# Two-layer attention and mixture-of-experts kernel: score groups placed together in the first attention, scores placed last in each step of the second

## The chip, the cores and the metric

The kernel runs on one core of a Trainium2 chip. The metric is device time in microseconds of one execution; the time of the kernel before is the median of three runs. A profile of one further execution shows what each engine did: TensorE (PE, with its weight loads as PEld), VectorE (DVE), ScalarE (ACT), GpSimd (POOL) and the DMA queue of SyncE (SP).

## What is computed

The input x is (2, 1024, 128) float32. Four blocks follow, each added to x. The two attentions are what the change touches; cut to what matters:

```python
x = x + attn0(layernorm(x)); x = x + moe(layernorm(x))
x = x + attn1(layernorm(x)); x = x + channel_mix(layernorm(x))

def attn0(X):                       # 16 heads, d = 64, 1024 tokens, 2 batch elements
    Q1, Q2, K1, K2 = halves of X @ Wq[h] and X @ Wk[h]; V = X @ Wv[h]
    P = softmax(Q1 @ K1.T * s) - lam * softmax(Q2 @ K2.T * s)
    O = P @ V                       # then Y = concat(O) @ Wo + bo, layer norm, * 0.2

def attn1(x):                       # 16 heads, d = 8, same tokens, masked keys
    O = softmax(Q @ K.T * s) @ V; return O @ Wo.T + bo
```

## The kernel before, in words

Each engine runs a list of instructions in a fixed order, written out by hand; semaphores tie them together. PSUM has eight banks of 512 float32 columns. In both attentions six banks hold scores, in turn in three pairs; the other two are `TRB`/`OT` (bank 6) and `MISC` (bank 7).

**First attention.** An item is one head of one batch element (32 of them, n = 2h + b), and `heads` runs the function `item` of each engine over them, with one more before and after. An item has eight steps s, each for 128 queries. A score group (`scores`, L1209 and L1210) is six fp16 matmuls on half the rows of the array, two at a time, into a pair of banks, once for p = 0 (the first softmax) and once for p = 1. For each, VectorE takes the negated row maximum (`maximum`, L825) and ScalarE the exponent with its row sum (`exponent`, L649). VectorE's `weigh` (L832, L834) works out the factor rho of the step before, and GpSimd (`subtract`, L511 and L513) scales the second softmax and subtracts it. Three steps later TensorE transposes the difference in two halves (`turn`, L1221, four 128x128 transposes each into bank 6), and ScalarE copies each half out (`keep_t`, L660). `turn` waits for the copy before it, since there is one bank.

Everything else of TensorE goes through MISC, in pieces named `first_misc` and `second_misc`: `values` (P times V, L1232), `to_out` (output projection, L1241), and the projections for the next item, `project_q` (L1245), `project_k` (L1251), `project_v` (L1259). Their users are on the other engines: `high` (ScalarE, L670) and `low` (VectorE, L842) split Q and K in two fp16 halves, `keep_v` (L866) keeps V, `normalise` (L850) divides the values' result, `add_out` (L860) adds the output. Since there is one MISC, each piece waits until the piece before has been read: in step 2 the second piece waits for `low` 0, in steps 5, 6, 7 for `low` 1, 2, 3; the first piece of step 1 and the second of step 4 wait for `normalise`; the first pieces of steps 5, 6, 7 for `add_out`, `keep_v` and `keep_v`; the first of step 2 for `add_out`.

VectorE's order in a step, which the change leaves alone, is: `normalise` (s = 1), `add_out` (s = 5) or `keep_v` (s = 6, 7); maximum of p = 0; `weigh`; `add_out` (s = 1), `normalise` (s = 4) or `low` (s = 2, 5, 6, 7); maximum of p = 1. ScalarE's order is: `high` (s = 2, 5, 6, 7), the copy of the first turn, exponent 0, the copy of the second turn, exponent 1.

TensorE's order in a step is:

```python
scores(n, b, u3, s, 0)
first_misc(h, b, s)
turn(..., 0)
scores(n, b, u3, s, 1)
turn(..., 1)
second_misc(h, b, s)
```

SyncE's queue carries the swap of QT's halves (`swap_q`, after `low` 0 and `low` 3), the reciprocal sums on their way over DRAM (`spread_r`) and the weights of the next head.

**Second attention.** A block n is four heads of one batch element, eight blocks of 32 steps t. In each step TensorE issues `maxima1` (L1463) for the next block, whose row maxima VectorE takes (L1110), and `scores1` (L1446) for this one, whose exponents ScalarE takes (L759); both are two fp16 matmuls into one pair of banks, and they take the three pairs in turn. So `maxima1` waits for the exponent of two steps before and `scores1` for the maximum of the step before. In odd steps `values1` (L1477, eight matmul records) follows for two steps that are done; it waits for the exponent of two steps before, and at t = 3 and t = 19 also for ScalarE's copy of `OT` (L737). At t = 3 and 19 come four small transposes (`spread1`, L1484), at t = 14 and 30 the output projection (`to_out1`, L1489). The block n = -1 has maxima only, the last block scores only; there `scores1` waits for the exponent of three steps before.

Of the kernel before, what the change touches and what calls it, by code (L numbers as in the profile page):

```python
# [28 lines left out]
def two_layers(nc, a, out):  # L29
    ctx = ExitStack()  # L30
    with ctx:
# [262 lines left out]
        def flags(h, b):  # L294

            if isinstance(h, int):
                n = 2 * h + b
                return 0 <= n - 1 < last0, 0 <= n < last0, 0 <= n + 1 < last0
            return True, True, True

        def at_least(eng, done, count):
            if not isinstance(count, int) or count > 0:
                eng.wait_ge(done, count)
# [314 lines left out]
        def _(act):  # L618
# [24 lines left out]
            def exponent(n, u3, s, p):  # L643
                u = 16 * n + 2 * s + p
                bank = 2 * ((u3 + 2 * s + p) % 3)
                act.wait_ge(s_max, u + 1)
                if p == 0:
                    at_least(act, s_tr_mm, 2 * (8 * n + s) - 6)
                A.activation((E1, E2)[p][s % 4], PS[:, bank:bank + 2, :].rearrange("p a b -> p (a b)"), ACT.Exp,  # L649
                             bias=nmx[:, 2 * s + p:2 * s + p + 1], scale=1.0,  # L650
                             accum_out=sums[:, s, p:p + 1]).then_inc(s_exp, 1)
# [20 lines left out]
            def item(h, b, u3):  # L672
                prv, own, nxt = flags(h, b)
                n = 2 * h + b
                for s in range(8):
                    if s == 1 and nxt and b == 1:
                        at_least(act, s_lo_ok, 4 * (n + 1))
                        A.activation(bcur[:, :], bqk[:, bass.ds(h + 1, 1), :].rearrange("p o i -> p (o i)"),
                                     ACT.Copy).then_inc(s_bc_ok, 1)
                    if s in (2, 5, 6, 7) and nxt:  # L680
                        high(n + 1, 1 - b, (2, 5, 6, 7).index(s), h + b + 1)
                    later = own if s >= 3 else prv
                    if later:
                        keep_t(n if s >= 3 else n - 1, (s + 5) % 8, 0)
                    if own:
                        exponent(n, u3, s, 0)
                    if later:
                        keep_t(n if s >= 3 else n - 1, (s + 5) % 8, 1)
                    if own:
                        exponent(n, u3, s, 1)  # L690

            heads(act, item)

            CT16 = MISC.bitcast(F16)[:, 0:HF]
# [464 lines left out]
        def _(pe):  # L1159
# [34 lines left out]
            def scores(n, b, u3, s, p):  # L1194


                u = 16 * n + 2 * s + p
                bank = 2 * ((u3 + 2 * s + p) % 3)
                if s == 0 and p == 0:
                    pe.wait_ge(s_lo_ok, 4 * n + 3)  # L1200
                    pe.wait_ge(s_qx_dma[0], 32 * (n + 1))
                if s == 4 and p == 0:
                    pe.wait_ge(s_lo_ok, 4 * n + 4)
                    pe.wait_ge(s_qx_dma[1], 32 * (n + 1))
                at_least(pe, s_exp, u - 2)
                top, bottom = (QT[b], QX[b]) if p == 0 else (QX[b], QT[b])
                q = slice(s * 128, s * 128 + 128)
                for j, (ql, kl) in enumerate(((0, 0), (0, 1), (1, 0))):
                    MM(PS[:, bank, :], top[0:64, ql, q], KT[b][0:64, p, kl, :], start=(j == 0), stop=(j == 2))  # L1209
                    mm = MM(PS[:, bank + 1, :], bottom[64:128, ql, q], KT[b][64:128, p, kl, :], start=(j == 0),  # L1210
                            stop=(j == 2))
                mm.then_inc(s_fill, 1)
# [49 lines left out]
            def first_misc(h, b, s):  # L1262
                prv, own, nxt = flags(h, b)
                n, m, p = 2 * h + b, 2 * h + b + 1, 1 - b
                if s == 0 and prv:
                    values(n - 1, p, 0, 2)
                if s == 1 and prv:
                    to_out(h + b - 1, n - 1, 0)
                if s == 2 and nxt:
                    at_least(pe, s_y_ok, 2 * n - 1)  # L1270
                    at_least(pe, s_lo_ok, 4 * m)
                    project_q(h + b, m, p, 0)
                if s == 3 and prv:
                    values(n - 1, p, 1, 1)
                if s == 4 and prv:
                    values(n - 1, p, 1, 3)
                if s == 5 and nxt:
                    at_least(pe, s_y_ok, 2 * n)
                    at_least(pe, s_lo_ok, 4 * m + 1)
                    project_k(h + b, m, p, 0)  # L1280
                if s == 6 and nxt:
                    pe.wait_ge(s_v_ev, 2 * m + 1)
                    project_k(h + b, m, p, 1)
                if s == 7 and nxt:
                    pe.wait_ge(s_v_ev, 2 * m + 2)
                    project_q(h + b, m, p, 1)

            def second_misc(h, b, s):
                prv, own, nxt = flags(h, b)
                n, m, p = 2 * h + b, 2 * h + b + 1, 1 - b  # L1290
                if s == 0 and prv:
                    values(n - 1, p, 0, 3)
                if s == 2 and prv:
                    pe.wait_ge(s_y_ok, 2 * n - 1)
                    if nxt:
                        pe.wait_ge(s_lo_ok, 4 * m + 1)
                    values(n - 1, p, 1, 0)
                if s == 3 and prv:
                    values(n - 1, p, 1, 2)
                if s == 4 and prv:  # L1300
                    to_out(h + b - 1, n - 1, 1)
                if s in (5, 6) and nxt:
                    pe.wait_ge(s_lo_ok, 4 * m + s - 3)
                    project_v(h + b, m, p, s - 5)
                if s == 7 and own:
                    at_least(pe, s_y_ok, 2 * n)
                    if nxt:
                        pe.wait_ge(s_lo_ok, 4 * m + 4)
                    values(n, b, 0, 0)
                    values(n, b, 0, 1)  # L1310

            def item(h, b, u3):
                prv, own, nxt = flags(h, b)
                n = 2 * h + b
                for s in range(8):
                    later = own if s >= 3 else prv
                    if own:
                        scores(n, b, u3, s, 0)
                    first_misc(h, b, s)
                    if later:  # L1320
                        turn(n if s >= 3 else n - 1, (s + 5) % 8, 0)
                    if own:
                        scores(n, b, u3, s, 1)
                    if later:
                        turn(n if s >= 3 else n - 1, (s + 5) % 8, 1)
                    second_misc(h, b, s)

            heads(pe, item)


# [156 lines left out]
            def to_out1(hf):  # L1487
                pe.wait_ge(s_on1_ok, hf + 1)
                MM(MISC, wo1[:, hf // 4, :], on[:, :], start=True, stop=True).then_inc(s_y1_mm, 1)  # L1489

            for n in range(-1, last1 + 1):
                own, nxt = 0 <= n < last1, n + 1 < last1
                for t in range(32):
                    if nxt:
                        maxima1(n + 1, t)
                    if own:
                        scores1(n, t)
                    if t == 1 and n >= 1:
                        values1(n - 1, 15)
                    if t % 2 == 1 and t > 1 and own:  # L1500
                        values1(n, t // 2 - 1)
                    if t == 3 and own:
                        if n >= 1:
                            pe.wait_ge(s_yc1_ok, 2 * n - 1)
                        spread1(2 * n + 1)
                    if t == 14 and n >= 1:
                        if own:
                            pe.wait_ge(s_ct_ev1, 2 * n + 2)
                        to_out1(2 * n - 1)
                    if t == 19 and nxt:  # L1510
                        if n >= 1:
                            pe.wait_ge(s_yc1_ok, 2 * n)
                        spread1(2 * (n + 1))
                    if t == 30 and own:
                        if nxt:
                            pe.wait_ge(s_ct_ev1, 2 * (n + 1) + 1)
                        to_out1(2 * n)


            pe.wait_ge(s_y1_ok, 4 * G1)  # L1520
# [55 lines left out]
```

## Time and profile before

| | before |
|---|---|
| median of 3 runs | 1957.23 us |
| lowest, highest | 1950.94, 1958.64 us |
| the profiled execution | 1955.24 us |
| its span | 1953.4 us |
| mean granted TensorE clock | 0.938 |
| busy TensorE, VectorE | 1628.1 us (83%), 1444.0 us (74%) |
| busy ScalarE, GpSimd | 1262.6 us (65%), 974.4 us (50%) |

The first attention lies from about 58 to 1262 us of the span, the second from about 1465 to 1897 us. Busy shares over the whole span hide that the two are bound by different things; the rows below show them one by one. The ends of matmuls are modelled, so the start of the next instruction is the better mark of when TensorE was free.

### The profile page before, as it was taken

To read this page: it belongs to the slowest core of one execution; us is meant where nothing else is said; L and a number is where in the kernel's file an instruction comes from. 1 tells how busy PE (TensorE), PEld (TensorE's weight loads), DVE (VectorE), ACT (ScalarE), POOL (GpSimd) and SP (SyncE) were. 2 spreads that over 40 slices of the span, in tenths; PEclk is the share of its full clock that TensorE was granted. 3 is DMA by queue.
4 is the path that set the end of the run, shared out by engine and by line. 5 is a ranking of instruction groups with operands and counts; after the bars stand their busy time and mean duration, and the time that the engine had idled before them with its cause. 6 is when DMAs were issued, how large, how long until landed. Compare 5 with 4: busy or idle time off the path is not lost.

```text
span 1953.4 us, 27210 instructions
## 1 busy us (share of the span) xinstructions
PE 1628.1 (83%) x9867; PEld 661.5 (34%) x9867; DVE 1444.0 (74%) x2199; ACT 1262.6 (65%) x2078; POOL 974.4 (50%) x637
## 2 busy tenths in 40 slices
PE   2899999999999999999999999833576777777763
PEld 1334444444434443444443444322441111111112
DVE  2678777777777877777777777596679777777608
ACT  1677777777777777777777777611052777777751
POOL 1577777777777777777777777720000011111110
PEclk8899999999999999999999999965685999999986
DMA  3111111111111111111111111000010000000000
GB/s 95 31 28 33 33 33 33 33 28 33 33 33 32 31 30 38 29 30 35 28 33 38 28 33 29 17 2 0 1 38 1 7 13 13 12 13 13 13 18 22
DMA packets 68107, 50.82 MB, mean 26 GB/s; under 512 B 27187, under 2 KB 56918, under 8 KB 67974
## 3 DMA queue, kind: packets, MB, share of 16 engines
q1 hardware_dynamic: 67974, 49.07, 11.1%
q8 instruction: 80, 1.31, 0.3%
q14 instruction: 53, 0.43, 0.1%
HBM read 28.79 MB, written 1.31 MB: 15 GB/s over the span
## 4 chain that ended last, share of the span: by engine, by line
PE 62%; issue 14%; DVE 13%; ACT 6%; POOL 2%; SPq 2%; DMA 0%; POOLq 0%; ACTq 0%; DVEq 0%
PE PS L1209 15%; PE PS L1221 14%; PE PS L1232 13%; DVE mxp L1110 4%; PE PS L1251 4%; PE PS L1241 3%; PE PS L1259 3%; ACT ering L649 3%; ACT va L660 2%; PE PS L1245 2%; DVE on L850 2%; PE PS L1477 2%; PE PS L1422 2%; DVE st L797 1%; POOL on L574 1%
## 5 line engine op out<-in xcount | busy, mean ns | idle before, releaser
L825 DVE TENSOR_REDUCE nmx<-PS 128x1 f32<-128x1024 f32 x512 | 625.4, 1222 | 212.1 <-PE PS L1210 206.1
L513 POOL TENSOR_TENSOR ering<-ering 128x1024 f32<-128x1024 f32 x256 | 603.7, 2358 | 21.4
L649 ACT ACTIVATE ering<-PS,nmx 128x1024 f32<-128x1024 f32 x512 | 572.6, 1118 | 2.9 <-DVE nmx L825 2.1
L511 POOL TENSOR_SCALAR ering<-ering,rho 128x1024 f32<-128x1024 f32 x256 | 286.6, 1119 | 300.9 <-DVE rho L834 300.9
L1209 PE MATMUL PS<-region 64*128 64x512 f16 x1536 | 420.4, 381 | 1.0 <-ACT ering L649 1.0
L1210 PE MATMUL PS<-region 64*128 64x512 f16 x1536 | 420.4, 381 | 0.0
L1110 DVE TENSOR_REDUCE mxp<-PS 128x2 f32<-128x1024 f32 x256 | 302.8, 1222 | 79.1 <-PE PS L1463 79.0
L1221 PE MATMUL PS<-ident,ering 128*128 128x128 f32 x2048 | 330.6, 284 | 11.4 <-ACT t L660 2.5
L759 ACT ACTIVATE ering<-PS 128x1024 f32<-128x1024 f32 x256 | 259.3, 1025 | 108.8 <-PE PS L1446 107.9
L1221 PEld LDWEIGHTS PS<-ident,ering 128*128 128x128 f32 x2048 | 222.0, 140 | 303.1 <-POOL ering L513 99.1
L660 ACT ACTIVATE t<-PS 128x512 f32<-128x512 f32 x256 | 152.6, 596 | 88.7 <-PE PS L1221 88.7
L1209 PEld LDWEIGHTS PS<-region 64*128 64x128 f16 x1536 | 105.4, 94 | 243.4 <-issue 96.8
L660 ACT ACTIVATE va<-PS 128x512 f32<-128x512 f32 x128 | 76.3, 596 | 131.9 <-PE PS L1221 131.9
L670 ACT ACTIVATE region<-PS,bcur 128x512 f16<-128x512 f32 x128 | 88.3, 690 | 93.6 <-PE PS L1251 50.8
L1477 PE MATMUL PS<-ering,acc 128*32 128x512 f32 x1024 | 137.3, 608 | 7.3 <-ACT osb L737 3.5
L842 DVE SCALAR_TENSOR_TENSOR region<-PS,bcur,region 128x512 f16<-128x512 f32 x128 | 96.1, 751 | 53.8 <-ACT region L670 46.6
L1232 PE MATMUL PS<-t,vslot 128*64 128x512 f32 x512 | 130.8, 611 | 0.0
L574 POOL TENSOR_TENSOR on<-osb,rcp 128x512 f32<-128x512 f32 x16 | 20.4, 1272 | 221.4 <-DMA rcp<-scr 221.4
L1446 PE MATMUL PS<-region 64*128 64x512 f16 x256 | 50.1, 388 | 86.2 <-DVE mxp L1110 74.6
L649 ACT ACTIVATION_READ_ACCUMULATOR ering<-PS,nmx 128x1 f32 x512 | 106.4, 208 | 0.0
L1210 PEld LDWEIGHTS PS<-region 64*128 64x128 f16 x1536 | 105.6, 95 | 0.0
L1245 PE MATMUL PS<-xT,wq_s 128*128 128x512 f32 x128 | 73.9, 660 | 14.5 <-POOL wq_s L504 14.0
(251 smaller groups left out, 1708.7 us busy)
## 6 DMA issues: line engine op xcount, KB each, us to landing
region<-region SPq DMA_DIRECT2D x128, 128.0 KB, 2.3
osb<-scr SPq DMA_DIRECT2D x32, 256.0 KB, 4.1
rcp<-scr SPq DMA_DIRECT2D x32, 256.0 KB, 4.1
rcp<-scr SPq DMA_DIRECT2D x64, 64.0 KB, 2.0
x<-in_L_attn_X SPq DMA_DIRECT2D x4, 256.0 KB, 3.7
wq_raw<-in_L_attn_Wq SPq DMA_DIRECT2D x16, 64.0 KB, 2.5
wk_s<-in_L_attn_Wk SPq DMA_DIRECT2D x16, 64.0 KB, 1.8
wo_s<-in_L_attn_Wo SPq DMA_DIRECT2D x32, 32.0 KB, 3.2
```

Of the source, the lines that this page charges most:

```text
L511: P.tensor_scalar(e2, e2, rho[:, s:s + 1], 1.0, ALU.mult, ALU.mult).then_inc(s_scl_ok, 1)
L513: P.tensor_tensor(e1, e1, e2, ALU.subtract).then_inc(s_sub_ok, 1)
L649: A.activation((E1, E2)[p][s % 4], PS[:, bank:bank + 2, :].rearrange("p a b -> p (a b)"), ACT.Exp, bias=nmx[:, 2 * s + p:2 * s + p + 1], s ...
L660: A.activation(PT[half][i][:, :, (s % 4) * 128:(s % 4) * 128 + 128], TRB.rearrange("p (k q) -> p k q", k=4), ACT.Copy).then_inc(s_tr_ev, 1)
L759: A.activation(ering[:, c % 8, :, :], PS[:, at:at + 2, :], ACT.Exp, scale=SCALE1).then_inc(s_exps1, 1)
L825: V.tensor_reduce(nmx[:, 2 * s + p:2 * s + p + 1], PS[:, bank:bank + 2, :].rearrange("p a b -> p (a b)"), AX.X, ALU.max, negate=True).then ...
L1110: V.reduce_max(part[:, hp:hp + 3:2, qt, kh:kh + 1], PS[:, at:at + 2, :], AX.X).then_inc(s_maxed1, 1)
L1209: MM(PS[:, bank, :], top[0:64, ql, q], KT[b][0:64, p, kl, :], start=(j == 0), stop=(j == 2))
L1210: mm = MM(PS[:, bank + 1, :], bottom[64:128, ql, q], KT[b][64:128, p, kl, :], start=(j == 0), stop=(j == 2))
L1221: mm = TR(TRB[:, j * 128:j * 128 + 128], E1[s % 4][:, k * 128:k * 128 + 128], ident[:, :])
L1232: mm = MM(MISC[64 * c:64 * c + 64, :], vslot[:, b, k, :], PT[half][k // 4][:, k % 4, :], start=(j == 0), stop=(j == 3))
L1477: mm = MM(OT[32 * i:32 * i + 32, :], vst[:, n % 2, k, i, :], ering[:, c % 8, i // 2, :], start=(k == 0), stop=(k == 7))
```

## The change

Three edits. On TensorE in the first attention a step is now first piece, score group 0, score group 1, turn 0, second piece, turn 1. On ScalarE both exponents stand between the copies of the two turns. On TensorE in the second attention the scores of a step come behind its values, its small transposes and its output projection. No instruction is added or removed.

```diff
--- before.py
+++ after.py
@@ -684,10 +684,9 @@
                         keep_t(n if s >= 3 else n - 1, (s + 5) % 8, 0)
                     if own:
                         exponent(n, u3, s, 0)
+                        exponent(n, u3, s, 1)
                     if later:
                         keep_t(n if s >= 3 else n - 1, (s + 5) % 8, 1)
-                    if own:
-                        exponent(n, u3, s, 1)
 
             heads(act, item)
 
@@ -1314,16 +1313,15 @@
                 n = 2 * h + b
                 for s in range(8):
                     later = own if s >= 3 else prv
+                    first_misc(h, b, s)
                     if own:
                         scores(n, b, u3, s, 0)
-                    first_misc(h, b, s)
+                        scores(n, b, u3, s, 1)
                     if later:
                         turn(n if s >= 3 else n - 1, (s + 5) % 8, 0)
-                    if own:
-                        scores(n, b, u3, s, 1)
+                    second_misc(h, b, s)
                     if later:
                         turn(n if s >= 3 else n - 1, (s + 5) % 8, 1)
-                    second_misc(h, b, s)
 
             heads(pe, item)
 
@@ -1493,8 +1491,6 @@
                 for t in range(32):
                     if nxt:
                         maxima1(n + 1, t)
-                    if own:
-                        scores1(n, t)
                     if t == 1 and n >= 1:
                         values1(n - 1, 15)
                     if t % 2 == 1 and t > 1 and own:
@@ -1515,6 +1511,8 @@
                         if nxt:
                             pe.wait_ge(s_ct_ev1, 2 * (n + 1) + 1)
                         to_out1(2 * n)
+                    if own:
+                        scores1(n, t)
 
 
             pe.wait_ge(s_y1_ok, 4 * G1)
```

## Rows read from the trace of the kernel before

**Rows 1.** Windows: stretch, length, busy (instructions) of PE, PEld, DVE, ACT, POOL, clock, DMA.

```profile
95.00:1208.00 1113.00, 1094.58 (x6629) 458.00 (x6630) 862.68 (x1244) 844.71 (x1553) 827.12 (x489) 1.00 0.15 32
601.07:638.60 37.53, 36.91 (x225) 15.40 (x224) 29.09 (x42) 28.53 (x53) 28.02 (x18) 1.00 0.14 35
1465.00:1500.00 35.00, 19.79 (x70) 3.56 (x66) 34.77 (x32) 1.87 (x2) 0.52 (x2) 0.50 0.00 1
1500.00:1870.00 370.00, 274.90 (x1984) 63.99 (x1982) 270.73 (x255) 268.25 (x286) 45.44 (x65) 0.99 0.05 12
```

**Rows 2.** Chain of waits, one step of the first attention: start, length, what.

```profile
622.86 0.43 PE PS L1221 x4
623.29 0.32 PE PS L1209
...
623.62 0.21 PE PS L1209
...
624.05 0.59 PE PS L1221 x4
```

**Rows 3.** Order of time, end of step 3, step 4: start, length, engine, line, operation.

```profile
633.01 1.08 PE L1232 MATMUL PS<-acc,vslot 128*64 128x512 f32 x4
...
634.02 0.39 PE L1209 MATMUL PS<-region 64*128 64x512 f16 x1
...
634.88 1.23 DVE L825 TENSOR_REDUCE nmx<-PS 128x1 f32<-128x1024 f32 x1 [1.13 <-PE PS L1210]
...
636.22 0.27 DVE L834 TENSOR_SCALAR rho<-sums,rr,cols 128x1 f32<-128x1 f32 x1
...
636.41 1.11 DVE L850 TENSOR_TENSOR on<-PS,rcp 128x512 f32<-128x512 f32 x1
...
637.62 1.08 PE L1241 MATMUL PS<-on,wo_s 128*128 128x512 f32 x2
...
638.63 0.39 PE L1209 MATMUL PS<-region 64*128 64x512 f16 x1
...
638.74 0.69 DVE L860 TENSOR_TENSOR yT<-yT,PS 128x512 f32<-128x512 f32 x1
```

**Rows 4.** Order of time, step 5 of the item before: low, maximum, projection, keep_v.

```profile
603.70 0.75 DVE L842 SCALAR_TENSOR_TENSOR region<-PS,bcur,region 128x512 f16<-128x512 f32 x1 [0.22 <-ACT region L670]
...
604.37 1.22 DVE L825 TENSOR_REDUCE nmx<-PS 128x1 f32<-128x1024 f32 x1
...
604.70 1.00 PE L1259 MATMUL PS<-wv_s,xT 128*128 128x64 f32 x8
...
605.74 0.42 DVE L866 TENSOR_TENSOR vslot<-PS,bv_b 128x256 f32<-128x256 f32 x1 [0.16 <-PE PS L1259]
```

**Rows 5.** Order of time, step 3: turn, its copy, the next turn.

```profile
631.08 0.66 PE L1221 MATMUL PS<-ident,ering 128*128 128x128 f32 x4
...
631.77 0.60 ACT L660 ACTIVATE t<-PS 128x512 f32<-128x512 f32 x1 [1.43 <-PE PS L1221]
...
632.42 0.66 PE L1221 MATMUL PS<-ident,ering 128*128 128x128 f32 x4
```

**Rows 6.** Order of time, second attention, one pair of steps.

```profile
1661.60 0.39 PE L1446 MATMUL PS<-region 64*128 64x512 f16 x2 [0.90 <-DVE mxp L1110]
...
1661.92 1.07 PE L1477 MATMUL PS<-ering,acc 128*32 128x512 f32 x8
1662.04 1.02 ACT L759 ACTIVATE ering<-PS 128x1024 f32<-128x1024 f32 x1 [0.48 <-PE PS L1446]
...
1662.92 0.39 PE L1463 MATMUL PS<-region,t 64*128 64x512 f16 x2
...
1663.35 2.36 DVE L1110 TENSOR_REDUCE mxp<-PS 128x2 f32<-128x1024 f32 x2 [0.52 <-PE PS L1463]
...
1664.64 0.39 PE L1446 MATMUL PS<-region 64*128 64x512 f16 x2 [0.89 <-DVE mxp L1110]
```

**Rows 7.** Order of time, second attention: copy of OT; exponents of the last block.

```profile
1654.99 0.59 ACT L737 ACTIVATE osb<-PS 128x512 f32<-128x512 f32 x1
...
1872.13 10.19 ACT L759 ACTIVATE ering<-PS 128x1024 f32<-128x1024 f32 x11 [0.56 <-PE PS L1446]
```

## The prediction

> **What bounds the kernel now.** I read the busy time by stretch first. In the steady part of the first attention TensorE is busy for 1094.6 of 1113 us at full clock, and one item (one head of one batch element, eight steps) takes 37.53 us, with TensorE busy for 36.91, VectorE for 29.1, ScalarE for 28.5 and GpSimd for 28.0 [rows 1]. So TensorE has next to no gap, and what counts for this part is two things: how long its instructions are, and whether the new order makes it wait. In the second attention no engine is full (275, 271 and 268 of 370 us): it is bound by a loop of waits. Then I read the chain of waits for what a piece of TensorE work costs behind another, and the order of time of single steps for the distance from each producer to its consumer.
>
> **Part 1, what the new order saves.** A step has two score groups (half-array fp16 matmuls), two turns (four full-array transposes each) and up to two pieces in the shared bank MISC. Four transposes cost 0.43 us behind full-array work and 0.59 behind score matmuls; the first score matmul costs 0.32, the ones behind it 0.21 [rows 2]. So a change of kind costs 0.11 to 0.16. I counted the changes in an item from the code: before (score, first piece, turn, score, turn, second piece) 41, after (first piece, score, score, turn, second piece, turn) 29. 12 x 0.14 = 1.7 us an item, 52 us over some 31 items. The Trainium skill says the same in "TensorEngine Tiling (Array Packing)", under "Key Properties": a change of tiling mode drains the array. By that rule alone the kernel would get faster; the trace agrees that the change of kind costs time.
>
> **Part 2, what the new order makes late.** VectorE's order is not touched: first maximum, the two small sums' operations, then (in seven of eight steps) one product for MISC's user, then the second maximum. Before the change TensorE had the first piece, a turn, the second score group and a turn between the first score group and the second piece, so the product was ready in time. I take step 4: score group at 634.02, its maximum at 634.88, rho at 636.22, the product `on` at 636.41 to 637.52, and the projection that needs it at 637.62, which is 3.6 us behind the score group's start and cost TensorE nothing [rows 3]. Now only the second score group and one turn stand between. I set up the step from its first score group at 0: second group at 0.74, turn at 1.38, its end 1.97. VectorE's product starts at 2.39 as before. A `low` takes 0.75 and so frees the second piece at 3.2 [rows 4]; a normalise takes 1.11 and frees it at 3.6 [rows 3]. TensorE stands still for 1.2 or 1.6 us, and everything it would have done then is queued behind. Step by step, in TensorE time from first score group to first score group:
> - Steps 5 and 6: the value projection waits for `low` until 3.2; it takes 0.84 to 1.0, the turn 0.43. Meanwhile the second maximum (from 3.06) and keep_v (0.42) end at 4.7, and the next first piece waits for keep_v because it reuses MISC. Plus 1.0 for that piece (the value group of [rows 3] takes 1.01): 5.7 each [rows 4].
> - Step 7: `low` until 3.2, two value groups of about 0.93, turn 0.59, the next value group 1.01: 6.65.
> - Step 0: one value group and both turns end at 3.57, but to_out now is the first piece of step 1 and needs normalise, which stands behind the second maximum (from 2.39 to 3.6) and ends at 4.7. Plus 1.0: 5.7.
> - Step 1: no second piece, so the second turn must wait for ScalarE's copy of the first, 1.34 after the first turn's start [rows 5]; with the query projection 4.1.
> - Step 2: `low` again, about 0.1 later since ScalarE is behind: 5.9.
> - Step 3 has no such piece and only saves: 4.6.
> - Step 4: to_out waits until 3.6, takes 1.0; the second maximum, then the addition (0.69) that frees MISC for the key projection end at 5.4. Plus 1.0: 6.45.
>
> The sum is 44.8 us an item against 37.53, the 1.7 already in it, so 7.3 more. The first item has no earlier item's pieces and the last no projections: about 3 us each. 30 x 7.3 + 6 = **225 us more**. Covers that are gone are named above. POOL: a difference is used a whole step after it is ready (on the engine's own rows it idles about a quarter of each item), so longer steps only give it room; no DMA is issued earlier or later against its user, and the swap of QT has a step and more of room. ScalarE has 28.5 us of work an item, 3.6 a step [rows 1], below every new step; only behind the short step 1 is it late, which is in the sum of step 2. Both banks' exponents of the step before are done when the score groups want their banks: nothing. Unknown is how exactly a stopped TensorE restarts; between nothing and the 0.2 us by which the loads of weights in these rows precede a restart, on six stops. I take nothing for the centre and widen by 0.25 a stop either way: 6 x 0.25 x 30 = 45 us.
>
> **Part 3, the second attention.** Two steps (even, odd) take 3.03 us: maxima group of the even step at 1662.92, its maximum from 1663.35, the odd step's scores at 1664.64 once that bank is read, then the values group (0.31 behind), and the next maxima group 1.00 later [rows 6]. In the new order the values group no longer stands behind that wait; the scores stand behind the values. The loop is now: end of the odd exponent, 0.05, maxima group, 0.32, values, 1.00, scores, 0.44, exponent, 1.02 = 2.83 [rows 6], 0.20 less for a pair. Against this: at t=3 and t=19 values wait for ScalarE's copy of OT (0.59 [rows 7]) and are followed by the small transposes, and the scores now stand behind all of it: about 1.4 more than a plain pair where before it was 0.4. At t=14 and t=30 to_out is before the scores, 0.28 against 0.1. A block of 16 pairs: 16 x 2.83 + 2 x 1.4 + 2 x 0.28 = 48.6, before 16 x 3.03 + 0.8 + 0.2 = 49.5. Seven blocks: -6 us. The last block has no maxima and ScalarE is its bound: 11 exponents in 10.19 us, 1.85 a pair [rows 7]. There the new loop (0.05 + 1.00 + 0.44 + 1.02 = 2.5) is the longer: 13 plain pairs x 0.65, about 8 us more. **Together +2**, between -6 (the last block hides it) and +15.
>
> **Sum.** The profiled execution took 1955.24 us (span 1953.4); 1955.2 + 225 + 2 = 2182; the median of the runs shown, 1957.23, is 2 above it. I say 2183. About 0.5% is what a measurement of this kernel can tell from no change.
>
> **Rivals.**
> - **The saved changes of kind win.** If the products were ready at 1.97 after the first score group, 52 us fall off TensorE: about 1905. It decides at the second piece of steps 2, 4, 5, 6 and 7; it holds only if VectorE finished its product 2.0 after that score group, and the rows have 3.1 and 3.5. Chance 0.04.
> - **Half of it is absorbed**: the stops in steps 0 and 5, 6 (the waits for keep_v and normalise at the head of the next step) vanish, because VectorE can start earlier than I think. Then some 3.5 us an item remain: 2065 to 2110. VectorE's idle time speaks for it, its fixed order against it. Chance 0.07.
> - **The clock falls.** Before the second attention TensorE, busy for 19.8 of 35 us, was granted 0.50; in it, 74% busy, 0.99 [rows 1]. New items are 80% busy with gaps up to 1.6 us, so I expect full clock. If it fell for good, its some 36 us of work an item would double: above 2800. If it fell only in the last block, 10 us. Chance of the first 0.03.
> - **More delay than I wrote**, through ScalarE in steps 1 and 2: 2250 to 2330. Chance 0.08.
> - The forecast: 0.78.
>
> **Range and chances.** The likeliest case with its bounds: 2183 - 45 - 6 and + 45 + 15, which is 2132 to 2243. It leaves about 0.2 out. Faster by over 0.5%: 0.04, the first rival. Within: 0.01. Slower: 0.95.
>
> **What the next profile would show.** An item of about 44.8 us; in it second pieces idle behind `low` (L842) and `on` (L850) for 1.2 and 1.6 us; TensorE about 80% busy in the first attention; VectorE and ScalarE with the same busy totals; the score groups six in a row with one 0.32; second attention pairs of 2.83 and, in the last block, 2.5. Wrong would be an item under 42 or over 48, or stops at other places than those listed.

## The result, and the profile after

The changed kernel takes 2202.35 us, median of four runs (2198.6 to 2213.89), the kernel before 1956.9 (four runs): ratio 1.126, 95% interval 1.124 to 1.128. It is 245 us slower. The profiled execution took 2204.14 us, its span is 2202.3. Two executions lie far above all others, 2879.72 us of the kernel with TensorE's order alone and 3144.76 us of the kernel before, and they are left out of every comparison.

| us | before | after | difference |
|---|---|---|---|
| start to the first transposes behind the first attention | 1268.4 | 1518.3 | +249.9 |
| from there to the first maximum of the second attention | 196.8 | 186.0 | -10.8 |
| from there to the last block's first scores | 383.5 | 375.8 | -7.7 |
| last block, first to last scores | 34.0 | 50.7 | +16.7 |
| the rest of the span | 70.7 | 71.5 | +0.8 |

The second line holds work that the change does not touch. The middle is the same in all the kernels compared here, and in their profiles this line came out between 186.0 and 197.2 us, so I do not count the 10.8 us as an effect of the change.

Windows of the changed kernel (stretch, length, busy and instructions of PE, PEld, DVE, ACT, POOL, granted clock, DMA share, GB/s): one item, the steady first attention, a stretch with a dip of the clock, and two stretches of the last block of the second attention.

```profile
711.25:756.56 45.31, 36.95 (x227) 15.95 (x226) 28.37 (x42) 29.64 (x53) 28.08 (x17) 1.00 0.13 28
95.00:1400.00 1305.00, 1067.86 (x6414) 457.40 (x6410) 813.32 (x1205) 847.45 (x1505) 799.93 (x473) 0.99 0.12 27
...
813.00:815.00 2.00, 2.00 (x6) 0.28 (x6) 0.00 (x0) 1.34 (x4) 0.80 (x1) 0.50 0.06 14
...
2085.00:2106.00 21.00, 17.45 (x75) 2.87 (x76) 0.25 (x1) 11.04 (x12) 1.27 (x1) 0.52 0.06 14
2106.00:2113.00 7.00, 4.28 (x28) 0.64 (x26) 0.00 (x0) 5.58 (x8) 1.27 (x1) 0.97 0.00 0
```

Against [rows 1]: an item is 45.31 us instead of 37.53 (37.62 when it is counted before, too, from score group to score group), and the busy times of the four engines in it are within 1.2 us of what they were. So the work has not grown; TensorE stands still. Who it waits for is in the waits of TensorE (engine and line waited for: us in total, times, longest):

```profile
PE PS L1240 <- DVE on L849: 77.6, 64, 1.5
PE PS L1258 <- DVE region L841: 73.1, 64, 1.6
...
PE PS L1231 <- issue: 34.5, 32, 1.2
...
PE PS L1231 <- ACT va L660: 25.8, 29, 0.9
PE PS L1220 <- ACT va L660: 22.0, 32, 0.7
```

L1240 is `to_out`, L1258 `project_v`, L1231 `values`, L1220 `turn`. In the kernel before `to_out` waited 16.2 us for the product in 33 places and `project_v` 3.1 us in 2; now it is 77.6 and 73.1 in 64 each. The two lines for `values` name "issue" and ScalarE, but they stand in steps 7 and 2, where the code's other wait is for `low` (VectorE); what is named had long been done (in step 7 `low` ends at 726.06 and `values` starts at 726.16). Together these waits for VectorE's products are some 211 us; `turn` waits 42 us for ScalarE's copies. Now the same step as in [rows 3], in order of time:

```profile
704.81 0.39 PE L1208 MATMUL PS<-region 64*128 64x512 f16 x1
...
705.68 1.23 DVE L824 TENSOR_REDUCE nmx<-PS 128x1 f32<-128x1024 f32 x1 [1.85 <-PE PS L1209]
...
707.20 1.07 DVE L849 TENSOR_TENSOR on<-PS,rcp 128x512 f32<-128x512 f32 x1
...
708.20 1.21 DVE L824 TENSOR_REDUCE nmx<-PS 128x1 f32<-128x1024 f32 x1
...
708.33 1.13 PE L1240 MATMUL PS<-on,wo_s 128*128 128x512 f32 x2 [1.46 <-DVE on L849]
...
709.50 0.69 DVE L859 TENSOR_TENSOR yT<-yT,PS 128x512 f32<-128x512 f32 x1
...
710.24 1.08 PE L1250 MATMUL PS<-xT,wk_s 128*64 128x512 f32 x4 [0.34 <-DVE yT L859]
...
711.25 0.39 PE L1208 MATMUL PS<-region 64*128 64x512 f16 x1
```

The distance from the score group's start to `on`'s start is 2.39 us, as before (704.81 to 707.20). But TensorE arrives early: it stood idle for 1.46 us before the output projection, which starts 3.52 us behind the score group (+3.52), and the key projection behind it waits for the addition, so that the next step starts at +6.44. Step 5, against [rows 4]:

```profile
713.64 0.74 DVE L841 SCALAR_TENSOR_TENSOR region<-PS,bcur,region 128x512 f16<-128x512 f32 x1
...
714.43 1.10 PE L1258 MATMUL PS<-wv_s,xT 128*128 128x64 f32 x8 [1.13 <-DVE region L841]
...
715.38 0.61 PE L1220 MATMUL PS<-ident,ering 128*128 128x128 f32 x4
...
715.58 0.42 DVE L865 TENSOR_TENSOR vslot<-PS,bv_b 128x256 f32<-128x256 f32 x1
...
716.06 1.08 PE L1250 MATMUL PS<-xT,wk_s 128*64 128x512 f32 x4
...
717.07 0.39 PE L1208 MATMUL PS<-region 64*128 64x512 f16 x1
```

`low` starts 2.39 us behind the score group (711.25), and TensorE stands idle for it before the value projection. Then `keep_v`, behind the second maximum, sets the start of the next piece. The step is 5.82 us. Score groups do not wait here: in the whole execution they do so twice, 1.6 us together, both in the first item.

The pair of steps of the second attention, against [rows 6]:

```profile
1901.72 0.39 PE L1461 MATMUL PS<-region 64*128 64x512 f16 x2 [0.69 <-ACT ering L758]
...
1902.04 1.06 PE L1475 MATMUL PS<-ering,acc 128*32 128x512 f32 x8
...
1903.04 0.39 PE L1444 MATMUL PS<-region 64*128 64x512 f16 x2
...
1903.47 1.94 ACT L758 ACTIVATE ering<-PS 128x1024 f32<-128x1024 f32 x2 [0.89 <-PE PS L1444]
...
1904.55 0.39 PE L1461 MATMUL PS<-region 64*128 64x512 f16 x2 [0.69 <-ACT ering L758]
```

From one maxima group of an odd step (L1461) to the next it is 2.83 us; a pair took 3.03 before. What the group waits for is the exponent; before, `scores1` waited for the maximum. The last block, first at half clock, then at full clock:

```profile
2099.00 1.94 PE L1475 MATMUL PS<-ering,acc 128*32 128x512 f32 x8 [0.69 <-ACT ering L758]
...
2100.87 0.61 PE L1444 MATMUL PS<-region 64*128 64x512 f16 x2
...
2101.51 1.94 ACT L758 ACTIVATE ering<-PS 128x1024 f32<-128x1024 f32 x2 [1.66 <-PE PS L1444]
...
2102.59 1.94 PE L1475 MATMUL PS<-ering,acc 128*32 128x512 f32 x8 [0.69 <-ACT ering L758]
...
2119.59 1.07 PE L1475 MATMUL PS<-ering,acc 128*32 128x512 f32 x8 [0.90 <-ACT ering L758]
...
2120.59 0.39 PE L1444 MATMUL PS<-region 64*128 64x512 f16 x2
...
2122.10 1.06 PE L1475 MATMUL PS<-ering,acc 128*32 128x512 f32 x8 [0.90 <-ACT ering L758]
```

A pair takes 3.59 us in the first stretch (2099.00 to 2102.59) and 2.51 in the second (2119.59 to 2122.10). In both, values, scores and one exponent stand one behind the other, so TensorE's instructions are in the pair at full length: from values to scores it is 1.87 us at half clock and 1.00 at full clock.

### The profile page after: what moved, and what is told of

It reads as the page before. It is cut to its first block, busy times and chain, and to the rows that moved or that the text cites. A ratio compares the mean times of both kernels' runs of the same rounds, so it can differ in the third digit from the quotient of the medians.

```text
span 2202.3 us, 27210 instructions
## 1 busy us (share of the span) xinstructions
PE 1639.2 (74%) x9867; PEld 669.8 (30%) x9867; DVE 1428.4 (65%) x2199; ACT 1285.5 (58%) x2078; POOL 973.5 (44%) x637
## 4 chain that ended last, share of the span: by engine, by line
PE 44%; DVE 30%; issue 18%; ACT 4%; POOL 2%; SPq 1%; DMA 0%; POOLq 0%; DVEq 0%; ACTq 0%
DVE nmx L824 12%; PE PS L1231 10%; PE PS L1208 10%; PE PS L1220 5%; PE PS L1258 3%; PE PS L1240 3%; PE PS L1250 3%; DVE on L849 3%; DVE region L841 2%; PE PS L1244 2%; DVE yT L859 2%; DVE mxp L1109 2%; PE PS L1475 2%; ACT ering L758 2%; PE PS L1420 1%
## 5 line engine op out<-in xcount | busy, mean ns | idle before, releaser
L649 ACT ACTIVATE ering<-PS,nmx 128x1024 f32<-128x1024 f32 x512 | 568.2, 1113 | 89.2 <-DVE nmx L824 87.1
L1208 PE MATMUL PS<-region 64*128 64x512 f16 x1536 | 383.5, 384 | 1.6 <-ACT ering L649 1.6
L1209 PE MATMUL PS<-region 64*128 64x512 f16 x1536 | 383.5, 384 | 0.0
L1220 PE MATMUL PS<-ident,ering 128*128 128x128 f32 x2048 | 331.1, 284 | 41.8 <-ACT va L660 22.0
L1109 DVE TENSOR_REDUCE mxp<-PS 128x2 f32<-128x1024 f32 x256 | 310.7, 1225 | 62.8 <-PE PS L1461 55.3
L758 ACT ACTIVATE ering<-PS 128x1024 f32<-128x1024 f32 x256 | 252.9, 1021 | 134.2 <-PE PS L1444 134.0
L1220 PEld LDWEIGHTS PS<-ident,ering 128*128 128x128 f32 x2048 | 221.5, 143 | 281.9 <-issue 195.8
L1208 PEld LDWEIGHTS PS<-region 64*128 64x128 f16 x1536 | 126.2, 95 | 332.8 <-ACT ering L649 149.0
L1475 PE MATMUL PS<-ering,acc 128*32 128x512 f32 x1024 | 143.3, 633 | 28.5 <-ACT osb L736 11.7
L1231 PE MATMUL PS<-t,vslot 128*64 128x512 f32 x512 | 131.0, 609 | 34.2 <-issue 33.1
L1240 PE MATMUL PS<-on,wo_s 128*128 128x512 f32 x128 | 72.0, 645 | 77.6 <-DVE on L849 77.6
L1258 PE MATMUL PS<-wv_s,xT 128*128 128x64 f32 x512 | 72.4, 286 | 73.1 <-DVE region L841 73.1
L1209 PEld LDWEIGHTS PS<-region 64*128 64x128 f16 x1536 | 126.2, 95 | 0.0
L1461 PE MATMUL PS<-region 64*128 64x512 f16 x256 | 53.8, 417 | 72.9 <-ACT ering L758 65.2
```

Of the source, the lines that this page charges most:

```text
L758: A.activation(ering[:, c % 8, :, :], PS[:, at:at + 2, :], ACT.Exp, scale=SCALE1).then_inc(s_exps1, 1)
L1109: V.reduce_max(part[:, hp:hp + 3:2, qt, kh:kh + 1], PS[:, at:at + 2, :], AX.X).then_inc(s_maxed1, 1)
L1220: mm = TR(TRB[:, j * 128:j * 128 + 128], E1[s % 4][:, k * 128:k * 128 + 128], ident[:, :])
L1231: mm = MM(MISC[64 * c:64 * c + 64, :], vslot[:, b, k, :], PT[half][k // 4][:, k % 4, :], start=(j == 0), stop=(j == 3))
L1475: mm = MM(OT[32 * i:32 * i + 32, :], vst[:, n % 2, k, i, :], ering[:, c % 8, i // 2, :], start=(k == 0), stop=(k == 7))
```

## The experiments

Both halves of the change were run, each single move of the first attention, and remedies for the wait that it brought. "Groups" are the two score groups of a step, "pieces" the MISC work, and each kernel differs from the kernel before by the diff shown, unless said otherwise. Repeated arguments are cut to `...` in the diffs. A range in brackets behind a ratio is its 95% interval.

**The two halves of the change.** First the second attention's edit alone:

```diff
-                    if own:
-                        scores1(n, t)
                     if t == 1 and n >= 1:
...
                         to_out1(2 * n)
+                    if own:
+                        scores1(n, t)
```

> The first attention as before, the second as changed. My account: the first seven blocks gain, 2.83 us a pair against 3.03, some 24.3 us a half block against 24.7, which is 6 us; the last block loses 8 us at full clock (2.5 us a pair against 1.85) and more where the clock is at 0.50 as it was for part of it in the changed kernel. Sum 1957 + 2 to + 10: 1959 to 1967 us. Rival: the second attention's share of the loss is larger than its own stretch shows and the first attention's smaller: then over 1975.

Measured: 1966.95 us, ratio 1.0049 (1.0022 to 1.0077). It is 9 us slower, at the upper end of the range. Its last block takes 50.7 us and its clock falls there at the same places as in the changed kernel.

The first attention's edits alone, TensorE's as below and ScalarE's as in the change:

```diff
+                    first_misc(h, b, s)
                     if own:
                         scores(n, b, u3, s, 0)
-                    first_misc(h, b, s)
+                        scores(n, b, u3, s, 1)
                     if later:
                         turn(..., 0)
-                    if own:
-                        scores(n, b, u3, s, 1)
+                    second_misc(h, b, s)
                     if later:
                         turn(..., 1)
-                    second_misc(h, b, s)
```

> The first attention as changed, the second as before. If the loss is in the first attention, item 45.3 us against 37.5, then 1957 + 237 = 2194 us, between 2185 and 2205. If a good part of the 245 us came from the second attention: under 2170.

Measured: 2196.18 us, ratio 1.1227 (1.1179 to 1.1275), 238 us more (two executions). The halves add up: 238 + 9 = 247 against 245.

**Where the second attention loses.** The scores last only in blocks that have maxima:

```diff
-                    if own:
+                    if own and not nxt:
                         scores1(n, t)
...
+                    if own and nxt:
+                        scores1(n, t)
```

> The first attention as before; in the second the scores stand last in blocks that have maxima, and at their old place in the last block. My account: the 6 us of seven blocks stay and the last block's 34 us are as before: 1957 - 6 = 1951 us, between 1948 and 1954, ratio 0.997. Rival: the gain of the seven blocks is only a shift that the last block gives back; then 1957 and no difference.

Measured: 1950.62 us, ratio 0.9960 (0.9941 to 0.9979). The gain of the seven blocks is real, and the last block alone turns it into a loss. Of all kernels run, this one is the fastest, but by less than 0.5%.

**TensorE's order without ScalarE's.** The kernel with the first attention's edits alone, with ScalarE's edit taken back:

```diff
                         exponent(n, u3, s, 0)
-                        exponent(n, u3, s, 1)
                     if later:
                         keep_t(..., 1)
+                    if own:
+                        exponent(n, u3, s, 1)
```

> The first attention with TensorE's new order and ScalarE's old one (copy, exponent, copy, exponent), the second attention as before. My account: TensorE's stops are for VectorE's low and normalise, so ScalarE's order hardly matters; the second exponent now waits for the copy of the second turn, which comes late, and is itself late for the next step's rho by little: 2190 to 2230 us. Rival: ScalarE's new order is what costs (both exponents hold up the copy that the next turn needs); then most of the loss goes and the kernel is under 2080.

Measured: 2201.03 us, a single execution, in the range expected. With TensorE's new order in place ScalarE's order makes no difference that this one execution could show (2201 against 2196).

**One move at a time.** The first piece ahead of the first group, groups apart:

```diff
+                    first_misc(h, b, s)
                     if own:
                         scores(n, b, u3, s, 0)
-                    first_misc(h, b, s)
```

> The kernel before, with one thing moved: the first piece of MISC stands ahead of the first score group; turns, second group and second piece keep their places, ScalarE and the second attention too. Theory 1 (the first maximum starts only when the first score group is done, and every piece of MISC waits for a product behind a maximum): the maximum starts 1.0 us later against the piece that frees MISC; steps 5 and 6 take 5.7 us, as in the changed kernel, since keep_v still stands behind the second maximum, steps 7 and 0 some 6.1 and 5.7, step 4 6.4: an item of some 43 to 44 us, 1957 + 190 = 2147 us, between 2100 and 2180. Theory 2 (the two score groups side by side are the cost): they are apart here, so no loss, 1957 within 1%.

Measured: 2152.96 us, ratio 1.0988 (1.0972 to 1.1004). This is inside the range. Its waits of TensorE in the first attention are again for VectorE's products, with the groups apart:

```profile
PE PS L1241 <- DVE on L850: 63.1, 64, 1.2
PE PS L1259 <- DVE region L842: 29.9, 64, 1.6
...
PE PS L1251 <- DVE yT L860: 23.4, 30, 0.8
...
PE PS L1251 <- DVE vslot L866: 16.5, 32, 0.5
```

So groups side by side aren't needed for most of the loss.

The second piece ahead of the second turn:

```diff
                         scores(n, b, u3, s, 1)
+                    second_misc(h, b, s)
                     if later:
                         turn(..., 1)
-                    second_misc(h, b, s)
```

> The kernel before, with one thing moved: the second piece of MISC stands ahead of the second turn; all else keeps its place. Theory 1: the piece starts 3.1 us behind the first score group instead of 3.6, so that a low (ready at 3.2) costs 0.1 to 0.2 in four steps and the normalise of step 4 (3.6) 0.5, and the second turn fills nothing any more: about 1 us an item, 1957 + 31 = 1988 us, between 1965 and 2010. Theory 2: no loss, since the groups are apart.

Measured: 1989.03 us, ratio 1.0165 (1.0143 to 1.0186): 30 us more, as expected.

The groups side by side, pieces in place:

```diff
                         scores(n, b, u3, s, 0)
+                        scores(n, b, u3, s, 1)
                     first_misc(h, b, s)
                     if later:
                         turn(..., 0)
-                    if own:
-                        scores(n, b, u3, s, 1)
-                    if later:
                         turn(..., 1)
```

> The kernel before, with one thing moved: the second score group stands right behind the first; both pieces of MISC keep their order behind them, and the two turns are left side by side. Theory 1: the first piece stays behind the first score group, so low is ready at 4.0 and the second piece starts at 4.2: no stop for VectorE. The cost is another: nothing stands between the turns, so each second turn waits 0.75 us for ScalarE's copy of the first (1.34 from turn to turn). Step 5.0 to 5.2, item 40.9 us, 1957 + 105 = 2062 us, between 2040 and 2085, TensorE's stops all at L1221. Theory 2 (groups side by side wait for their banks): the stops are at L1209, behind ScalarE's exponents, and the loss is 200 us or more.

Measured: 2097.78 us, ratio 1.0712 (1.0696 to 1.0728): 139 us, outside the range that I gave (83 to 128), with the stops where they were expected:

```profile
PE PS L1221 <- ACT va L660: 96.6, 128, 0.8
PE PS L1221 <- ACT t L660: 88.6, 128, 1.1
```

```profile
706.80 0.39 PE L1209 MATMUL PS<-region 64*128 64x512 f16 x1
...
708.20 1.08 PE L1251 MATMUL PS<-xT,wk_s 128*64 128x512 f32 x4
...
709.21 0.66 PE L1221 MATMUL PS<-ident,ering 128*128 128x128 f32 x4
...
710.56 0.66 PE L1221 MATMUL PS<-ident,ering 128*128 128x128 f32 x4 [0.69 <-ACT t L660]
...
711.05 1.00 PE L1259 MATMUL PS<-wv_s,xT 128*128 128x64 f32 x8
```

The first fence is its waits, the second a step of 5.19 us: groups, key projection, turn, second turn, value projection. The value projection follows the second turn at once: no wait for `low`. From turn to turn it is 1.35 us, as expected (1.34). The item took 42.15 us where 40.9 was expected; which part of that sum was short is not shown.

ScalarE's order alone:

```diff
                         exponent(n, u3, s, 0)
+                        exponent(n, u3, s, 1)
                     if later:
                         keep_t(..., 1)
-                    if own:
-                        exponent(n, u3, s, 1)
```

> The kernel before, with one thing moved: ScalarE's second exponent stands ahead of the copy of the second turn. Theory 1: the copy ends at 6.2 where the next first turn wants it at 6.4 counted from the first score group, so there is hardly a wait but in the short step 1 and where high stands behind the copy: 0 to 0.7 us an item, 1957 + 10, between 1955 and 1980 us. Rival: the copy is the bound and each step loses 0.4 or more: 2050 or above.

Measured: 1988.22 us, ratio 1.0147 (1.0126 to 1.0168): a miss by 8 us above the range. It costs 0.8 us an item (38.44 us from score group to score group against 37.62); the waits show 24.7 us at the first turn (L1220) in 32 places, 0.74 in step 2, behind the short step 1. I had named the place and not priced it.

The four moves cost 194, 30, 139 and 30 us alone, 393 together, and 238 in one kernel. They are no terms of a sum: in the changed kernel the second piece between the turns covers the copy whose wait costs 139 us alone. `turn` waits 185 us for copies in that kernel and 42 in the changed one.

**Taking the wait away on VectorE's side.** These three start from the changed kernel and move only VectorE's instructions, so that the products no longer stand behind maxima. First `low` and the `normalise` of step 4:

```diff
+                    if s == 4 and prv:
+                        normalise(n - 1, 1)
+                    if s in (2, 5, 6, 7) and nxt:
+                        low(n + 1, 1 - b, (2, 5, 6, 7).index(s))
                     if own:
                         maximum(n, u3, s, 0)
...
-                    if s == 4 and prv:
-                        normalise(n - 1, 1)
-                    if s in (2, 5, 6, 7) and nxt:
-                        low(n + 1, 1 - b, (2, 5, 6, 7).index(s))
```

> The changed kernel, with VectorE's low (steps 2, 5, 6, 7) and the normalise of step 4 ahead of the step's first maximum; nothing else is moved. Theory 1 (TensorE stops for VectorE's products in MISC): the stops at the second pieces of steps 2, 4, 5, 6 and 7 go, but in steps 5 and 6 the next first piece still waits for keep_v, and behind step 4 for the addition, both behind the second maximum, so that only steps 2, 7 and a part of 4 gain: 2.8 us an item, 2202 - 85 = 2117 us, between 2095 and 2140. Theory 2 (the two score groups side by side wait for exponents to free their banks): the maxima come later, so the banks come free later, and the kernel is at 2200 or above.

Measured: 2140.64 us, ratio 1.0933 (1.0913 to 1.0953), 62 us less than the changed kernel, 0.6 us outside the range. As expected the waits moved to the next first piece, behind `keep_v` and the addition:

```profile
PE PS L1244 <- DVE vslot L865: 41.6, 32, 1.3
PE PS L1250 <- DVE vslot L865: 38.5, 32, 1.4
PE PS L1250 <- DVE yT L859: 33.2, 30, 1.1
```

Not as expected, step 2 kept its 6.0 us: there `low` waits 2.34 us for ScalarE's `high` (711.18 to 711.87, group at 709.56), which is late behind step 1.

Then `keep_v`, the other `normalise` and the second addition go ahead of the second maximum too, in the step in which their matmuls end. On top of the edit before:

```diff
-                    if s == 1 and prv:
-                        normalise(n - 1, 0)
-                    if s == 5 and prv:
-                        add_out(n - 1, 1 - b, 1)
-                    if s in (6, 7) and nxt:
-                        keep_v(h + b, n + 1, 1 - b, s - 6)
...
                         weigh(...)
+                    if s == 0 and prv:
+                        normalise(n - 1, 0)
...
+                    if s == 4 and prv:
+                        add_out(n - 1, 1 - b, 1)
+                    if s in (5, 6) and nxt:
+                        keep_v(h + b, n + 1, 1 - b, s - 5)
                     if own:
                         maximum(n, u3, s, 1)
```

> As the run before, and keep_v, the other normalise and the addition also stand ahead of the second maximum of the step in which their matmuls end. Theory 1: no piece in MISC waits behind a maximum any longer, TensorE is the bound again with 12 changes of kind an item less: an item of about 36.8 us, 1957 - 22 + 9 (second attention) = 1944 us, between 1930 and 1965. Theory 2: above 2150, since nothing is done about the banks.

Measured: 2155.42 us, ratio 1.1022 (1.0998 to 1.1046). A clear miss, 211 us above the forecast, and 15 us more than with `low` and one `normalise` moved alone; against the changed kernel it is 47 us less. And with the last block of the second attention in its old order:

```diff
+                    if own and not nxt:
+                        scores1(n, t)
                     if t == 1 and n >= 1:
...
-                    if own:
+                    if own and nxt:
                         scores1(n, t)
```

> As the run before, with the last block of the second attention in its old order. Theory 1: 9 to 15 us less than the run before, about 1930 us, faster than the kernel before by 1 to 1.5%. Theory 2: above 2140.

Measured: 2144.3 us, ratio 1.0959 (1.0941 to 1.0976). The last block gave its 11 us; the first attention did not get better. Order of time in step 5 of this kernel (group at 736.72):

```profile
736.83 1.11 ACT L649 ACTIVATE ering<-PS,nmx 128x1024 f32<-128x1024 f32 x1 [1.02 <-DVE nmx L824]
...
737.93 0.59 ACT L660 ACTIVATE t<-PS 128x512 f32<-128x512 f32 x1
738.41 0.69 ACT L670 ACTIVATE region<-PS,bcur 128x512 f16<-128x512 f32 x1
...
738.66 0.63 PE L1220 MATMUL PS<-ident,ering 128*128 128x128 f32 x4 [0.47 <-ACT t L660]
739.13 0.75 DVE L841 SCALAR_TENSOR_TENSOR region<-PS,bcur,region 128x512 f16<-128x512 f32 x1 [2.34 <-ACT region L670]
...
739.94 1.10 PE L1258 MATMUL PS<-wv_s,xT 128*128 128x64 f32 x8 [0.65 <-DVE region L841]
```

ScalarE is the next in line: the second exponent of the step before starts only at 736.83, since its maximum is now late; behind it stands the copy of the turn, for which TensorE's first turn waits 0.47 us, then `high`, for which `low` waits 2.34 us, for which the value projection waits 0.65. So, last, the same kernel with ScalarE's old order:

```diff
                         exponent(n, u3, s, 0)
-                        exponent(n, u3, s, 1)
                     if later:
                         keep_t(..., 1)
+                    if own:
+                        exponent(n, u3, s, 1)
```

> The run e7 (all of VectorE's products early, last block of the second attention in its old order) with ScalarE's old order: copy, exponent, copy, exponent. In e7 TensorE's stops have moved: the first turn of steps 5, 7, 1 and 2 waits 0.42 to 0.47 us for ScalarE's copy of the turn before, which stands behind both exponents. Theory 1b (VectorE first, ScalarE next: with the maxima late, the exponents are late, and the copy behind them): these waits go, those for low behind high stay; 4 x 0.45 x 31 = 55 us less than e7's 2144, about 2090, between 2060 and 2125. If the copy's place does not matter: 2144, or more, since high now stands behind the second exponent.

Measured: 2075.66 us, ratio 1.0594 (1.0567 to 1.0620), 69 us less than the run before it and inside the range. Half of the loss of the first attention is gone by now. The largest wait left in it is the value projection's for `low`, behind `high` (44.3 us); those of `values` (26.7 and 21.4 us), `turn` (22.0) and `to_out` (20.9) follow. An order that takes the saved changes of kind without a new wait was not found.

## Why the prediction was right

The forecast was 2183 us, 2132 to 2243; the measured 2202 is 19 above it. The path and the waits were the ones forecast. That the total came so near is in part luck: both attentions were put too low, by 25 and 7 us, and the middle, which the change does not touch, came out 11 us shorter in the profile. By its own steps:

- **Mechanism.** TensorE stops at second pieces and at the next first pieces for VectorE's products in MISC: shown by the waits (1.46 us before the output projection and 1.13 before the value projection, where 1.6 and 1.2 were forecast), by the first piece's move alone, which costs 194 us with the groups apart, and by VectorE's reordering, which moves the stops.
- **The steps.** Forecast and measured, steps 5, 6, 7, 0, 1, 2, 3, 4: 5.7, 5.7, 6.65, 5.7, 4.1, 5.9, 4.6, 6.45 against 5.82, 5.86, 6.70, 5.70, 4.19, 6.00, 4.60, 6.44. Sum 44.8 against 45.31. The missing 0.5 lies in steps 5, 6, 1 and 2, about a tenth each. The restart of a stopped TensorE was put at nothing and is a tenth: from the value projection to its turn it is 0.95 us behind a stop (714.43 to 715.38), and 0.85 in the kernel with `low` moved first, where the same projection stands between the same turns without a stop. But it does not set the length of step 5: there `keep_v` ends at +4.75 and the key projection starts at +4.81, where 4.7 was taken. So how much of the 0.5 is the restart is not shown.
- **The count.** I took 30 items and 6 us for both ends. From the first item's step 5 to the last's there are 31 full rounds, and the two ends together grew by 4 us: 5 us or so too few. 31 times 7.7 is 239 of the 249.9.
- **The clock.** A fall for good was a rival and did not come; short falls did, and so did that rival's smaller case, a fall in the last block of the second attention. In seven places of the first attention the granted clock was 0.50 for a few us (813 to 815 in the windows above), and each cost 1.0 to 1.5 us (the item around 814 took 1.3 us longer), some 9 us in all. Before there was none.
- **Second attention.** +2 was forecast, with -6 to +15; the profile has +9, the run of that half alone +9. The pair of 2.83 and the pair of 2.51 are exact, the seven blocks gave 8 us instead of 6. The term that was mis-sized is the last block, 17 us instead of 8: for 21 us of it the clock was at 0.52, where a pair takes 3.59 us, and five such pairs (the fifth in a second, short fall) instead of pairs of 2.51 are 5.4 of the missing 9 us. The rest I have not split; the sum had 13 plain pairs of 16 and put the growth of the other three at nothing.
- **The rivals.** That 12 changes of kind less would win is refuted for this order, not as a mechanism: step 3, the one without a new wait, went from 4.70 to 4.60. The Trainium skill says in "TensorEngine Tiling (Array Packing)", "Key Properties", that changing the tiling mode drains TensorE. The trace agrees that a change costs time; it is a tenth of a microsecond beside a wait of a whole one. That half would be absorbed is refuted: steps 5, 6 and 0 took 5.82, 5.86 and 5.70 us, with VectorE's order as it was.

## What to carry to other kernels

Before moving work on a full engine, write down for each piece how far behind its producer's start its consumer now stands, and what the consumer's own order puts ahead of the product. The order that looks fragmented may be what covers a round trip: here 3.6 us from score group to output projection, against 0.1 us a change of kind. When one engine's wait is taken away, look at the next engine in the loop before expecting the gain: moving VectorE's products brought back 62 and 47 of the 245 us, and the next wait was for ScalarE.

## What was not expected of the hardware

- The clock of TensorE dipped to its half level (0.50, 1.2 GHz) in the middle of the first attention, seven times for a few microseconds, six of them in the stretch where the engine was busy for 1068 of 1305 us with stops of up to 1.5 us. The kernel with the first attention's edits alone had such dips too. The kernel before, busy for 1095 of 1113 us, had none, and neither had the one with the first piece ahead, busy for 1095 of 1265 us (95 to 1360) with stops of up to 1.2 us. What brings them on is not shown. In the last block of the second attention it was at 0.52 over 21 us (17.45 of them busy) and at 0.97 in the next 7 us (4.28 busy). The kernel with the second attention's edit alone shows the same fall in that block; in the kernel before its clock was 1.00 throughout.
- A stopped TensorE pays about 0.1 us more than its wait. From the value projection to its turn it is 0.95 us behind a stop and 0.85 without one. Behind the stop the first weight load starts together with the matmul (714.43); where the projection did not wait, in the kernel with the groups side by side, it starts 0.10 us ahead (710.95 and 711.05).
